# Projections and shared maxima of a decoder block's main loop in two 64-row phases, beside score halves of the other row half

## The chip, the cores and the metric

One Trainium2 chip, one core of it. The metric is the device time of one execution in microseconds (us); less is better. Before the change the median of 3 runs is 760.02 us (757.07 to 762.93).

## The reference

A decoder block on `x` (32 batches, 56 tokens, 128 features) with a context of 32 x 1500 x 128:

```python
x = layernorm(x + linear_attention(x))
x = layernorm(x + cross_attention(x, ctx))
x = layernorm(x + ffn(x))

qh = (q @ Wq.T + bq)   # 16 heads of 8
kh = (k @ Wk.T + bk)
vh = (v @ Wv.T + bv)
scores = qh @ kh.T / sqrt(8)
out = softmax(scores) @ vh
```

Nearly all the time goes to the cross attention: for each of 32 batches, 1500 keys are projected to K and V, and 16 heads x 56 queries meet 1500 keys.

## The kernel before

The first stage (up to some 135 us) does the linear attention of all batches and, beside it, the K and V of the first batches. Then comes the **main loop**, one body for each of the 32 batches b; bodies 0 and 1 and the last two stand alone, the 28 between are a hardware loop of 14 passes, two bodies (u = 0, then u = 1) in each. A last stage does the feed-forward part.

In body b TensorE (PE) does, in a written-out order of six **steps** m = 0..5:

- **Scores** (line 1066) of batch b: 12 key tiles of 125 keys, two in each step. The 16 heads are stored in two halves of 64 partitions, so a tile is 4 pairs of matmuls: 64 rows x 128 columns of weights, 112 moving columns, one of the pair on the upper and one on the lower 64 rows of the array, at the same time. ScalarE (ACT) takes the exponent (line 756) of each half of a tile (4 x 112 columns) from one of three PSUM banks into `probs`.
- **PV** (lines 1083 and 1089): `probs` times V in fp32, in tiles of 128 x 32, two key tiles at the end of each step, one step late.
- **K2** (line 954), the projection of batch b + 2 to K: three units of 500 keys, each three fp16 matmuls of 128 rows and 500 columns (high and low parts of operands). ACT adds the bias (line 776, `k32`); GpSimd (POOL) casts it to fp16 (`kcast`, line 580) and forms the rest (`ksub`, line 586).
- **V** (line 962), the projection of batch b + 1 to V: three units, each 12 fp16 matmuls of 128 rows and 128 columns; ACT copies (line 765).
- **Maxima** (line 974): products of q and K whose row maxima VectorE (DVE) takes (line 1313, 672 ns each). There are 21 for each batch: 12 of the last ones of batch b + 1 ("M1") and 9 of the first ones of batch b + 2 ("M2"). A maximum is 500 columns; six of the seven row blocks need 64 rows only, and these go in pairs on the two row halves; the middle block (`SHARED`, r = 3) needs all 128 rows.
- **X** (line 978): turns the maxima; they are placed into `q_diag` by DMA before the next body's scores. In bodies with u = 0 there are also **T, Z, Y** (lines 982, 986, 989), which finish the output of the two batches before.

K2, V, maxima, X, T, Z and Y write into a **ring** of four PSUM banks in the order of the table `PLAN`; before a unit is written, PE waits until the unit that last held the bank has been read (`release`, line 942). A score of tile t waits for the exponents of tile t - 1's first half (line 1062), since there are three score banks.

POOL's order in a body (line 653): split chunks 0 and 1 of the context of b + 2 into high and low parts (`split`, line 557), `diag_q` of b + 1, chunk 2, `kcast` 0, `max_q` of b + 2, `kcast` 1 and 2, three `ksub`. The splits of b + 2 begin when the last V of batch b has been formed, since that used the same buffer.

SyncE (SP) moves K through DRAM into its stacked form (`store_k`, `load_k`), places the maxima and loads the context.

A PE matmul's tile is 64 x 128 for scores and unshared maxima, 128 x 128 for K2, V, shared maxima, T, Z and Y, and 128 x 32 for PV.

Of the kernel before, what the change touches and what calls it, by code (L numbers as in the profile page):

```python
# [34 lines left out]
ACT = mybir.ActivationFunctionType  # L35
# [62 lines left out]
def settle(engine, counter):  # L98
# [13 lines left out]
U1_SHIFT = 3  # L112
LATE_STACK = 4
PAIR_KINDS = ("T", "Z", "Y")
VW = 48
M_ORDER = ((3, 0), (0, 0), (4, 0), (1, 0), (5, 0), (2, 0), (6, 0), (0, 1), (4, 1), (1, 1), (5, 1), (3, 1),
           (2, 1), (6, 1), (0, 2), (4, 2), (1, 2), (5, 2), (3, 2), (2, 2), (6, 2))
PAIRS = (1, 3, 5, 7, 9, 12, 14, 16, 19)
SHARED = MB // 2
PLAN = ((("M1", "M1", "M1", "K2"), ("M1", "M1"), ()),  # L120
        (("M1", "M1", "V"), ("M1", "M1"), ()),
        (("M1", "K2", "M1", "M1"), (), ()),
        (("M2", "K2", "X"), ("M2", "M2", "T"), ()),
        (("V", "Z"), ("M2", "M2"), ()),
        (("M2", "M2", "V", "Y"), ("M2", "M2"), ()))
O_COPY = (0, 1)

def unit_plan(u):

    made = {"M1": EARLY_M}
    steps = []
    for parts in PLAN:
        step = []
        for kinds in parts:
            units = []
            for kind in kinds:
                if kind in PAIR_KINDS and u:
                    continue
                units.append((kind, made.get(kind, 0)))  # L140
                made[kind] = made.get(kind, 0) + 1
            step.append(units)
        steps.append(step)
    assert made["M1"] == NM and made["M2"] == EARLY_M and made["V"] == made["K2"] == KC
    return steps
# [7 lines left out]
def ring_slots():  # L153

    rounds = [[unit for step in unit_plan(u) for part in step for unit in part] for u in range(2)]
    return [{unit: (k + u * U1_SHIFT) % RING for k, unit in enumerate(units)} for u, units in enumerate(rounds)]

def left_in_ring(slots, u, s1, s2, before):

    left = {}
    for (kind, i), slot in slots[u].items():
        if active(kind, s1, s2, before):
            left[slot] = (kind, i)
    return left
# [76 lines left out]
def decoder_block(nc, ctx_dram, x_dram, pack_dram, out_dram, m):  # L242
# [4 lines left out]
    plans = [unit_plan(u) for u in range(2)]  # L247

    with ExitStack() as stack:
# [89 lines left out]
        init, o_zeroed = sem("init"), sem("o_zeroed")  # L339
        INIT = 2 + 4  # L340
# [33 lines left out]
        with nc.Block() as block:  # L374
# [125 lines left out]
            def _(pool):  # L500
# [204 lines left out]
            def _(act):  # L705
# [44 lines left out]
                def exp(b, t):  # L750
                    for half in range(2):
                        k = 2 * t + half
                        act.wait_ge(s_ready, b * 2 * KT + k + 1)
                        if half == 0:
                            wait_past(act, pv_done, b * KT + t - PBUF + 1)
                        nc.scalar.activation(probs[0:KP, t % PBUF, half * 2 * GC:(half + 1) * 2 * GC],  # L756
                                             scores[k % RING_AT][0:KP, 0:2 * GC], ACT.Exp, scale=SCALE).then_inc(p_ready, 1)

                def v_copy(n, i, u, bank):
                    act.wait_ge(ready["V"], n * 3 + i + 1)  # L760
                    if i == 0:
                        wait_past(act, pv_done, (n - 1) * KT)
# [43 lines left out]
                def body(b, u, s1, s2):  # L806

                    def copies(units):
                        for kind, i in units:
                            bank = ring[slots[u][kind, i]]  # L810
                            if kind == "V" and s2:
                                v_copy(b + 1, i, 1 - u, bank)
                            if kind == "X" and s2:
                                m_copy(b + 1, bank)
                            if kind == "K1" and s2:
                                k_copy(b + 1, i, bank)
                            if kind == "K2" and s1:
                                k_copy(b + 2, i, bank)

                    for m, (one, two, three) in enumerate(plans[u]):  # L820
                        exp(b, 2 * m)
                        if not s2 and 2 * m in X2T_STEPS:
                            x2_T(X2T_STEPS.index(2 * m))
                        copies(one)
                        exp(b, 2 * m + 1)
                        copies(two + three)
# [32 lines left out]
            def _(pe):  # L859
# [88 lines left out]
                def unit(kind, i, n, u, bank, before):  # L948
# [15 lines left out]
                    elif kind in ("M1", "M2"):  # L964
                        r, c = M_ORDER[i]
                        if i % MB == 0:
# [90 lines left out]
                def score(b, t, u):  # L1057
                    if t == 0:
# [3 lines left out]
                    wait_past(pe, p_ready, b * 2 * KT + 2 * t - 1)  # L1062
                    for g in range(G):
                        for half in range(2):
                            rows = slice(HALF * half, HALF * half + HALF)
                            mm = nc.tensor.matmul(scores[(2 * t + half) % RING_AT][:, g * PAIR:(g + 1) * PAIR],  # L1066
                                                  k_stack[u][rows, g, t * KP:t * KP + P],
                                                  q_diag[u][rows, g * PAIR:(g + 1) * PAIR], start=True, stop=True)
                            if g == G - 1:
                                mm.then_inc(s_ready, 1)  # L1070

                def pv(b, t, u):
# [6 lines left out]
                    pe.wait_ge(p_ready, b * 2 * KT + 2 * t + 2)  # L1079
# [17 lines left out]
                def body(b, pair, u, s1, s2, before, held):  # L1097
# [3 lines left out]
                    def go(units):  # L1101
                        for kind, i in units:
                            if active(kind, s1, s2, before):
                                n, slot = of_batch(kind, b, pair), slots[u][kind, i]
                                if kind in ("M1", "M2") and i in PAIRS:
                                    release(held[slots[u][kind, i + 1]])
                                unit(kind, i, n, u if kind in ("K2", "M2") else 1 - u, ring[slot], held[slot])
                                held[slot] = (kind, i, n)

                    for m, (one, two, three) in enumerate(plans[u]):  # L1110
                        score(b, 2 * m, u)
                        if not s2 and 2 * m in X2T_STEPS:
                            x2_T(X2T_STEPS.index(2 * m))
                        go(one)
                        score(b, 2 * m + 1, u)
                        go(two)
# [6 lines left out]
                        go(three)  # L1123
# [64 lines left out]
            def _(dve):  # L1188
# [211 lines left out]
                def body(b, pair, u, s1, s2, before):  # L1400

                    def reduce(units):
                        for kind, i in units:
# [141 lines left out]
```

## Time and profile before

| | |
|---|---|
| median of 3 runs | 760.02 us (757.07 to 762.93) |
| profiled execution, span from first to last instruction | 747.8 us |
| around the span (median less span) | 12.2 us |
| PE busy / DVE / ACT / POOL | 90% / 78% / 73% / 63% |
| mean granted TensorE clock | 0.970 |
| two bodies in the steady part of the loop | 35.19 us |

The profiled execution's own time is not given beside its span; the median less the span stands for what lies around it. Busy counts the time from a matmul's start to its modelled end, so PE at 90% need not be PE at its peak: how far apart the starts of matmuls stand tells more. A line number is that of the listing above.

### The profile page before, as it was taken

How to read it: one execution, taken by the hardware profiler on the slowest of the kernel's cores; microseconds unless marked ns; L12 is line 12 of the kernel's file. 1: busy time of each engine (PE TensorE's matmuls, PEld its weight loads, DVE VectorE, ACT ScalarE, POOL GpSimd, SP SyncE). 2: the span in 40 equal slices, each digit the busy share in tenths (PEclk: the TensorE clock that was granted, in tenths of full speed). 3: DMA queues.
4: the chain of work that ended last, by engine and by line, in shares of the span. 5: the costliest groups of instructions: out<-in, count | busy, mean ns of one | idle time of the engine just before them, and what ended most of it. 6: DMA issues, size and time to landing. Idle time of an engine off the chain costs nothing.

```text
span 747.8 us, 33172 instructions
## 1 busy us (share of the span) xinstructions
PE 672.6 (90%) x12468; PEld 431.4 (58%) x12468; DVE 586.6 (78%) x1139; ACT 548.7 (73%) x1123; POOL 471.6 (63%) x507
## 2 busy tenths in 40 slices
PE   6779864999899999999999999999999999998883
PEld 3456531566566666666666666666666666666553
DVE  5768976887588888888887878888788888885597
ACT  4537523788688888888888888888788888887751
POOL 6625424477477777777676777667777777723464
PEclk9989986899999999999999999999999999999997
DMA  7203402579767767687877776777767677761001
GB/s 217 83 2 101 89 16 81 88 172 210 148 103 151 179 142 148 146 164 145 160 146 155 151 145 144 145 166 150 180 155 150 144 160 150 127 109 15 1 1 49
DMA packets 39405, 93.20 MB, mean 125 GB/s; under 512 B 7880, under 2 KB 14536, under 8 KB 39368
## 3 DMA queue, kind: packets, MB, share of 16 engines
q1 hardware_dynamic: 39368, 92.69, 59.1%
q8 instruction: 25, 0.41, 0.3%
q14 instruction: 12, 0.10, 0.1%
HBM read 66.06 MB, written 26.54 MB: 124 GB/s over the span
## 4 chain that ended last, share of the span: by engine, by line
PE 70%; DVE 14%; issue 7%; ACT 6%; DMA 1%; POOL 1%; ACTq 0%; DVEq 0%; POOLq 0%
PE psum L1066 13%; PE psum L1083 12%; PE psum L974 11%; PE psum L962 10%; PE psum L1089 9%; DVE mx L1313 5%; PE psum L954 4%; ACT probs L756 3%; PE psum L905 2%; ACT k L776 1%; DVE rden L1241 1%; PE psum L891 1%; PE psum L982 1%; PE psum L920 1%; DVE k_stack L1452 1%
## 5 line engine op out<-in xcount | busy, mean ns | idle before, releaser
L1313 DVE TENSOR_REDUCE mx<-psum 128x1 f32<-128x500 f32 x672 | 423.8, 673 | 85.8 <-PE psum L974 83.5
L756 ACT ACTIVATE probs<-psum 125x448 f32<-125x448 f32 x768 | 376.0, 544 | 85.9 <-PE psum L1066 84.7
L974 PE MATMUL psum<-kh,q_max 64*128 64x500 f16 (+1 forms) x672 | 149.0, 383 | 15.0 <-DVE mx L1313 14.9
L1083 PE MATMUL psum<-probs,v_ext 125*32 125x112 f32 x3072 | 149.3, 266 | 0.5 <-issue 0.5
L1066 PE MATMUL psum<-q_diag,k_stack 64*128 64x112 f16 x3072 | 143.0, 212 | 3.3 <-ACT probs L756 2.2
L1089 PE MATMUL psum<-probs,v_ext 125*32 125x112 f32 x3072 | 144.6, 260 | 0.0
L580 POOL CAST kh<-k 128x500 f16<-128x500 f32 x96 | 57.9, 603 | 120.4 <-ACT k L776 112.0
L1066 PEld LDWEIGHTS psum<-q_diag,k_stack 64*128 64x128 f16 x3072 | 85.0, 95 | 67.8 <-ACT probs L756 38.7
L568 POOL TENSOR_TENSOR c_hl<-c_in,c_hl 128x500 f16<-128x500 f32 x96 | 110.6, 1152 | 7.7
L586 POOL TENSOR_TENSOR kl<-k,kh 128x500 f16<-128x500 f32 x96 | 107.4, 1148 | 0.0
L1083 PEld LDWEIGHTS psum<-probs,v_ext 125*32 125x32 f32 x3072 | 74.1, 109 | 38.8 <-issue 26.0
L566 POOL CAST c_hl<-c_in 128x500 f16<-128x500 f32 x96 | 60.0, 625 | 47.4 <-PE psum L962 44.5
L1089 PEld LDWEIGHTS psum<-probs,v_ext 125*32 125x32 f32 x3072 | 87.3, 110 | 0.0
L962 PE MATMUL psum<-WvH,c_hl 128*128 128x128 f16 x768 | 76.1, 221 | 0.0
L974 PEld LDWEIGHTS psum<-kh,q_max 64*128 64x128 f16 (+1 forms) x672 | 39.2, 94 | 61.8 <-DVE mx L1313 35.8
L962 PE MATMUL psum<-WvL,c_hl 128*128 128x128 f16 x384 | 69.5, 219 | 3.3 <-issue 3.3
L776 ACT ACTIVATE k<-psum,pack 128x500 f32<-128x500 f32 x96 | 65.1, 679 | 7.5 <-PE psum L954 6.2
L962 PEld LDWEIGHTS psum<-WvH,c_hl 128*128 128x128 f16 x768 | 55.7, 98 | 20.5 <-DVE mx L1313 15.4
L765 ACT COPY v_ext<-psum 125x512 f32<-125x512 f32 x96 | 56.7, 590 | 4.0 <-PE psum L962 4.0
L954 PE MATMUL psum<-c_hl,WkH 128*128 128x500 f16 x192 | 56.6, 376 | 0.5 <-ACT mT L771 0.3
L607 POOL TENSOR_TENSOR q_max<-qh,pack 128x896 f16<-128x896 f32 (+1 forms) x32 | 54.1, 1691 | 1.4 <-ACT qh L747 1.4
L962 PEld LDWEIGHTS psum<-WvL,c_hl 128*128 128x128 f16 x384 | 37.8, 98 | 3.5 <-issue 3.5
(143 smaller groups left out, 681.2 us busy)
## 6 DMA issues: line engine op xcount, KB each, us to landing
k_stack<-k_halves SPq DMA_DIRECT2D x192, 187.5 KB, 6.3
c_in<-ctx_in SPq DMA_DIRECT2D x32, 750.0 KB, 5.2
k_halves<-kh SPq DMA_DIRECT2D x32, 375.0 KB, 4.8
k_halves<-kl SPq DMA_DIRECT2D x32, 375.0 KB, 5.5
q_stack<-q_halves SPq DMA_DIRECT2D x32, 64.0 KB, 2.4
q_diag<-mT SPq DMA_DIRECT2D x64, 0.8 KB
q_diag<-mT SPq DMA_DIRECT2D x64, 0.1 KB
out<-x_all SPq DMA_DIRECT2D x8, 112.0 KB
```

The costliest lines, as they stand in the source:

```text
L566: nc.gpsimd.tensor_copy(c_hl[:, buf, 0, keys], c_in[:, buf, keys]).then_inc(c_hi, 1)
L568: nc.gpsimd.tensor_tensor(c_hl[:, buf, 1, keys], c_in[:, buf, keys], c_hl[:, buf, 0, keys], ALU.subtract).then_inc(c_split, 1)
L586: nc.gpsimd.tensor_tensor(kl[u][:, keys], k32[:, keys], kh[u][:, keys], ALU.subtract).then_inc(kl_done, 1)
L756: nc.scalar.activation(probs[0:KP, t % PBUF, half * 2 * GC:(half + 1) * 2 * GC], scores[k % RING_AT][0:KP, 0:2 * GC], ACT.Exp, scale=SCALE ...
L776: nc.scalar.activation(k32[:, i * CH:(i + 1) * CH], bank[:, 0:CH], ACT.Identity, bias=w("bk")).then_inc(k32_done, 1)
L954: last = nc.tensor.matmul(bank[:, 0:CH], wt[:, :], c_hl[:, u, part, i * CH:(i + 1) * CH], start=(k == 0), stop=(k == 2))
L962: last = nc.tensor.matmul(bank[:, j * P:(j + 1) * P], c_hl[:, u, part, at:at + P], wt[:, :], start=(k == 0), stop=(k == 2))
L974: last = nc.tensor.matmul(bank[:, 0:CH], q_max[u][rows, r * P:(r + 1) * P], kh[u][rows, c * CH:(c + 1) * CH], start=True, stop=True)
L1066: mm = nc.tensor.matmul(scores[(2 * t + half) % RING_AT][:, g * PAIR:(g + 1) * PAIR], k_stack[u][rows, g, t * KP:t * KP + P], q_diag[u][ro ...
L1083: nc.tensor.matmul(O[32 * j:32 * j + 32, 0:2 * N], v_ext[u][0:KP, v:v + 32], probs[0:KP, t % PBUF, at:at + 2 * N], start=(t == 0), stop=(t ...
L1089: last = nc.tensor.matmul(O[32 * j:32 * j + 32, 2 * N:GC], v_ext[u][0:KP, v:v + 32], probs[0:KP, t % PBUF, at + 2 * N:at + GC], start=Fals ...
L1313: dve.tensor_reduce(mx[:, r * KC + c:r * KC + c + 1], bank[:, 0:CH], AX.X, ALU.max).then_inc(mx_done, 1)
```

## The change

Everything that was 128 rows deep in the loop, but for X, T, Z, Y and PV, is cut into two phases of 64 rows. A K2 unit is 3 matmuls on the upper 64 rows (phase 0) and 3 on the lower (phase 1), accumulating in one bank; a V unit 12 and 12; a shared maximum 1 and 1. While such a phase holds one row half, the other row half holds four score matmuls or a maximum. Scores change from "two halves of one tile" to "one half of two tiles": in step m, scores j = 0 and 1 are the lower half of tiles 2m and 2m + 1, scores j = 2 and 3 their upper half. New semaphores `k_low`, `v_low`, `m_high` make phase 1 wait for phase 0.

Each step holds exactly one projection unit: V0, K2 0, K2 1, K2 2, V1, V2 (`UNITS_OF`). Steps 0 to 2 hold four M1 maxima each, steps 3 to 5 two unshared and one shared M2 maximum each. X goes from the middle of step 3 to its end. Ring bank 0 holds projections alone, banks 1 to 3 the maxima and T, Z, Y, X.

The tables:

```diff
+UNITS_OF = (("V", 0), ("K2", 0), ("K2", 1), ("K2", 2), ("V", 1), ("V", 2))
+def maxima_of(m):
+    if m < M1_STEPS:
+        at = EARLY_M + 4 * m
+        return "M1", (at, at + 1, at + 2, at + 3)
+    at = 3 * (m - M1_STEPS)
+    return "M2", (at, at + 2, at + 1, at + 2)
...
+        table = {unit: 1 + k % (RING - 1) for k, unit in enumerate(ring_users(u))}
+        table["X", 0] = table[maxima_of(X_STEP)[0], maxima_of(X_STEP)[1][2]]
+        table.update({unit: 0 for unit in UNITS_OF})
```

GpSimd's body:

```diff
+                        max_q(b + 2, u)
                         kcast(b + 2, 0, u)
-                        max_q(b + 2, u)
                         kcast(b + 2, 1, u)
+                        ksub(b + 2, 0, u)
                         kcast(b + 2, 2, u)
-                        ksub(b + 2, 0, u)
```

ScalarE's body:

```diff
+                    for m in range(KT // 2):
+                        kind, i = UNITS_OF[m]
+                        if m == X_STEP + 1 and s2:
+                            m_copy(b + 1, ring[slots[u]["X", 0]])
+                        exp(b, m, 0)
+                        exp(b, m, 1)
+                        exp(b, m, 2)
+                        if kind == "V" and s2:
+                            v_copy(b + 1, i, 1 - u, ring[0])
+                        if kind == "K2" and s1:
+                            k_copy(b + 2, i, ring[0])
...
+                        exp(b, m, 3)
```

TensorE:

```diff
+                def score(b, m, j, u, g):
+                    k, t, half = 4 * m + j, 2 * m + j % 2, 1 - j // 2
...
+                    if g == 0:
+                        wait_past(pe, p_ready, b * 2 * KT + k - 2)
...
+                def k_part(n, i, u, half, part):
+                    rows = slice(HALF * half, HALF * half + HALF)
+                    wt, of = ((WkH, 0), (WkH, 1), (WkL, 0))[part]
...
+                    if half == 1 and part == 0:
+                        pe.wait_ge(k_low, (n - 2) * KC + i + 1)
+                    mm = nc.tensor.matmul(ring[0][:, 0:CH], wt[rows, :], c_hl[rows, u, of, i * CH:(i + 1) * CH],
+                                          start=(half == 0 and part == 0), stop=(half == 1 and part == 2),
...
+                    def beside_score(m, j, half, part, kind, i, live):
+                        for g in range(G):
+                            if live and kind == "V":
+                                v_part(b + 1, i, 1 - u, half, 4 * part + g)
+                            if live and kind == "K2" and g == 0:
+                                k_part(b + 2, i, u, half, part)
+                            score(b, m, j, u, g)
...
+                    for m in range(KT // 2):
...
+                        if live:
+                            own(kind, i)
+                        beside_score(m, 0, 0, 0, kind, i, live)
+                        bank = own(top, one) if counted else None
+                        beside_maximum(0, 1, kind, i, live, top, one, bank)
+                        beside_score(m, 1, 0, 2, kind, i, live)
+                        if counted:
+                            second = own(top, two)
+                            maximum(b + 1 if top == "M1" else b + 2, two, 1 - u if top == "M1" else u, 1, second)
+                        for g in range(G):
+                            score(b, m, 2, u, g)
+                        bank = own(top, three) if counted else None
+                        beside_maximum(1, 0, kind, i, live, top, three, bank)
+                        beside_score(m, 3, 1, 1, kind, i, live)
...
+                            bank = own(top, four)
+                        beside_maximum(1, 2, kind, i, live, top, four, bank)
...
                         if m:
                             pv(b, 2 * m - 2, u)
                             pv(b, 2 * m - 1, u)
```

`beside_maximum(half, part, ...)` issues the next third of the projection (one `k_part`, or four `v_part`) with one maximum on the other row half behind its first matmul; `own` is `release` and the note of who holds the bank. VectorE takes the maxima in the order in which PE forms them, `o_copy` at the end of step 0, T, Z and Y behind the maxima of steps 3, 4 and 5.

What PE's rows look like in a step with a K2 unit, before (the loop's first body, from the scores of tile 4 to PV; lines of the listing above; REGISTER_ALU works out what a wait is for):

```order
L1066 MATMUL psum<-q_diag,k_stack 128x112 x8
L946 REGISTER_ALU
L974 MATMUL psum<-kh,q_max 128x500
L946 REGISTER_ALU
L952 REGISTER_ALU
L954 MATMUL psum<-c_hl,WkH 128x500 x2
L954 MATMUL psum<-c_hl,WkL 128x500
L946 REGISTER_ALU x2
L974 MATMUL psum<-kh,q_max 128x500 x2
L90 REGISTER_ALU
L1066 MATMUL psum<-q_diag,k_stack 128x112 x8
L1079 REGISTER_ALU
```

And after, the first part of such a step (L1107 is K2, L1093 the scores, L1143 a maximum):

```order
L1104 REGISTER_ALU
L1107 MATMUL psum<-c_hl,WkH 128x500
L90 REGISTER_ALU
L1093 MATMUL psum<-q_diag,k_stack 128x112 x4
L972 REGISTER_ALU
L1107 MATMUL psum<-c_hl,WkH 128x500
L1143 MATMUL psum<-kh,q_max 128x500
L1107 MATMUL psum<-c_hl,WkL 128x500
L90 REGISTER_ALU
L1093 MATMUL psum<-q_diag,k_stack 128x112 x4
L972 REGISTER_ALU
L1143 MATMUL psum<-kh,q_max 128x500
```

The three K2 matmuls no longer follow each other: each is now a 64-row one and has four scores or a maximum behind it on the other row half, and a step reads one K2 unit twice in this way.

POOL at the end of a body of the loop, before (L568 is a split, L580 `kcast`, L607 `max_q`, L586 `ksub`):

```order
L568 TENSOR_TENSOR c_hl<-c_in,c_hl 128x500
L90 REGISTER_ALU x2
L580 CAST kh<-k 128x500
L607 ISA
L607 TENSOR_TENSOR q_max<-qh,pack 128x896
L580 CAST kh<-k 128x500 x2
L586 TENSOR_TENSOR kl<-k,kh 128x500 x3
```

And after (L599 a split, L638 `max_q`, L611 `kcast`, L617 `ksub`):

```order
L599 TENSOR_TENSOR c_hl<-c_in,c_hl 128x500
L635 REGISTER_ALU
L638 ISA
L638 TENSOR_TENSOR q_max<-qh,pack 128x896
L90 REGISTER_ALU
L611 CAST kh<-k 128x500 x2
L617 TENSOR_TENSOR kl<-k,kh 128x500
L611 CAST kh<-k 128x500
L617 TENSOR_TENSOR kl<-k,kh 128x500 x2
```

`max_q` now stands ahead of the first `kcast`, and one `ksub` between the second and the third.

## Rows read from the trace of the kernel before

**Rows 1.** The page: the chain that ended last, shares by engine

```profile
PE 70%; DVE 14%; issue 7%; ACT 6%; DMA 1%; POOL 1%; ACTq 0%; DVEq 0%; POOLq 0%
```

**Rows 2.** Windows, one pass of the loop: us, busy (x records) by engine, PEclk

```profile
375.49:392.33 16.84, 16.62 (x356) 10.77 (x355) 13.82 (x25) 14.68 (x32) 12.68 (x14) 1.00 0.68 147
392.33:410.68 18.35, 17.69 (x363) 11.43 (x363) 14.84 (x30) 14.80 (x32) 12.69 (x14) 1.00 0.79 154
```

**Rows 3.** Waits in that pass, longest of ACT: who for whom, total us, times, longest

```profile
ACT probs L756 <- PE psum L1066: 5.3, 12, 1.1
```

**Rows 4.** Timeline, PE in a step with V: start, us, line, form, count

```profile
404.05 0.37 PE L1066 MATMUL psum<-q_diag,k_stack 64*128 64x112 f16 x8
...
404.26 0.37 PE L974 MATMUL psum<-kh,q_max 64*128 64x500 f16 x2
...
404.57 0.28 PE L962 MATMUL psum<-WvH,c_hl 128*128 128x128 f16 x2
...
405.19 0.22 PE L962 MATMUL psum<-WvL,c_hl 128*128 128x128 f16 x1
...
405.34 0.37 PE L1066 MATMUL psum<-q_diag,k_stack 64*128 64x112 f16 x8
...
405.55 0.37 PE L974 MATMUL psum<-kh,q_max 64*128 64x500 f16 x2
...
405.85 0.40 PE L1083 MATMUL psum<-probs,v_ext 125*32 125x112 f32 x8
...
406.76 0.37 PE L1066 MATMUL psum<-q_diag,k_stack 64*128 64x112 f16 x8
```

**Rows 5.** Timeline, PE around a K2 unit

```profile
401.02 0.69 PE L974 MATMUL psum<-kh,q_max 64*128 64x500 f16 x3
...
401.55 0.58 PE L954 MATMUL psum<-c_hl,WkH 128*128 128x500 f16 x2
...
401.97 0.37 PE L954 MATMUL psum<-c_hl,WkL 128*128 128x500 f16 x1
...
402.28 0.37 PE L1066 MATMUL psum<-q_diag,k_stack 64*128 64x112 f16 x8
```

**Rows 6.** Timeline, ACT: exponents, K2's copy, V's copy

```profile
402.38 0.68 ACT L776 ACTIVATE k<-psum,pack 128x500 f32<-128x500 f32 x1
...
402.96 0.97 ACT L756 ACTIVATE probs<-psum 125x448 f32<-125x448 f32 x2
...
404.53 0.98 ACT L756 ACTIVATE probs<-psum 125x448 f32<-125x448 f32 x2 [0.60 <-PE psum L1066]
...
405.45 0.59 ACT L765 COPY v_ext<-psum 125x512 f32<-125x512 f32 x1
...
405.93 0.99 ACT L756 ACTIVATE probs<-psum 125x448 f32<-125x448 f32 x2
```

**Rows 7.** Timeline, DVE: maxima one after another

```profile
401.43 3.08 DVE L1313 TENSOR_REDUCE mx<-psum 128x1 f32<-128x500 f32 x5 [0.17 <-PE psum L974]
```

**Rows 8.** Timeline, POOL: a split, diag_q, the next split, kcast, max_q

```profile
400.83 0.60 POOL L566 CAST c_hl<-c_in 128x500 f16<-128x500 f32 x1
...
402.61 0.94 POOL L595 TENSOR_TENSOR q_diag<-q_stack,pack 128x448 f16<-128x448 f32 x1
...
403.49 0.60 POOL L566 CAST c_hl<-c_in 128x500 f16<-128x500 f32 x1
...
405.25 0.60 POOL L580 CAST kh<-k 128x500 f16<-128x500 f32 x1
...
405.81 1.69 POOL L607 TENSOR_TENSOR q_max<-qh,pack 128x896 f16<-128x896 f32 x1
```

**Rows 9.** Timeline, PE in the loop's first pass; the page's queue of instruction packets

```profile
200.04 0.23 PE L962 MATMUL psum<-WvL,c_hl 128*128 128x128 f16 x1 [3.33 <-issue]
...
q8 instruction: 25, 0.41, 0.3%
```

**Rows 10.** The DMA queues between 220 and 660 us, all instruction packets

```profile
q14 instruction: 2, 0.02, 0.0%
```

More of the change, by code:

```diff
@@ L126 @@
[L126 to L145, printed above, removed]
+HIGH_ORDER = ((4, 0), (5, 0), (6, 0), (4, 1), (5, 1), (6, 1), (4, 2), (5, 2), (6, 2))
@@ new lines, with ring_users @@
+M_ORDER = maxima_order()
+CHUNK_FIRST = tuple(min(i for i in range(NM) if M_ORDER[i][1] == c) for c in range(KC))
+def maxima_of(m):
[4 more added lines that the diff above has]
+    return "M2", (at, at + 2, at + 1, at + 2)
+def ring_users(u):
+    users = []
+    for m in range(KT // 2):
+        kind, (one, two, three, four) = maxima_of(m)
+        users += [(kind, one), (kind, two), (kind, three)]
+        if four != two:
+            users.append((kind, four))
+        if u == 0 and m in (T_STEP, Z_STEP, Y_STEP):
+            users.append((("T", "Z", "Y")[m - T_STEP], 0))
+    return users
@@ L1099, in body @@
                     held = dict(held)
[L1101 to L1108, printed above, removed]
@@ L1110, in body, with own @@
-                    for m, (one, two, three) in enumerate(plans[u]):
-                        score(b, 2 * m, u)
+                    def own(kind, i):
+                        slot = slots[u][kind, i]
+                        release(held[slot])
+                        held[slot] = (kind, i, of_batch(kind, b, pair))
+                        return ring[slot]
+                    def beside_score(m, j, half, part, kind, i, live):
[5 more added lines that the diff above has]
+                            score(b, m, j, u, g)
@@ new lines, in beside_maximum @@
+                    def beside_maximum(half, part, kind, i, live, top, at, bank):
+                        n, of = (b + 1, 1 - u) if top == "M1" else (b + 2, u)
+                        if live and kind == "V":
+                            v_part(b + 1, i, 1 - u, half, 4 * part)
+                        if live and kind == "K2":
+                            k_part(b + 2, i, u, half, part)
+                        if bank is not None:
+                            maximum(n, at, of, 1 - half, bank)
+                        for g in range(1, G):
+                            if live and kind == "V":
+                                v_part(b + 1, i, 1 - u, half, 4 * part + g)
@@ new lines, in body @@
+                    for m in range(KT // 2):
+                        kind, i = UNITS_OF[m]
+                        live = active(kind, s1, s2, before)
+                        top, (one, two, three, four) = maxima_of(m)
+                        counted = active(top, s1, s2, before)
+                        if live:
[12 more added lines that the diff above has]
+                        beside_score(m, 3, 1, 1, kind, i, live)
+                        if not counted:
+                            bank = None
+                        elif four == two:
+                            bank = second
+                        else:
+                            bank = own(top, four)
+                        beside_maximum(1, 2, kind, i, live, top, four, bank)
@@ L1112, in body @@
                         if not s2 and 2 * m in X2T_STEPS:
                             x2_T(X2T_STEPS.index(2 * m))
-                        go(one)
-                        score(b, 2 * m + 1, u)
-                        go(two)
+                        for last_of, name in ((T_STEP, "T"), (Z_STEP, "Z"), (Y_STEP, "Y")):
+                            if m == last_of and u == 0 and before:
+                                slot = slots[u][name, 0]
+                                unit(name, 0, pair - 1, 0, ring[slot], held[slot])
+                                held[slot] = (name, 0, pair - 1)
@@ L1400, in body @@
                 def body(b, pair, u, s1, s2, before):
[L1402 to L1406 removed]
+                    for m in range(KT // 2):
+                        top, (one, two, three, four) = maxima_of(m)
+                        for i in sorted({one, two, three, four}):
+                            if top == "M1" and s2:
+                                m_max(b + 1, i, ring[slots[u][top, i]])
                                 if i == NM - 1:
```

173 lines of the change are left out of this document (100 added, 73 removed).

## The prediction

> **What bounds the kernel now.** I read the page's chain first, then windows over one pass of the loop, then the waits, and last the timeline of each engine in one step. The chain runs 70% through PE [rows 1]. A pass of the loop (two bodies) takes 16.84 + 18.35 = 35.19 us, the same in pass after pass, and PE shows busy in nearly all of it, while ACT and DVE show 14 to 15 us in each body and POOL 12.7 [rows 2]. ACT's longest wait is for PE's scores [rows 3]: the other engines wait for PE.
>
> "Busy" hides what PE loses, so look at the starts. Two K2 matmuls stand 0.42 us before the third, 0.21 each for 500 columns [rows 5]; eight scores in pairs take 404.05 to 404.26, 0.21; the twelve V matmuls start every (405.19 - 404.57) / 11 = 0.056 [rows 4]. But from a pair of maxima (500 columns) to the first V matmul it is 404.26 to 404.57, 0.31; from the last V matmul to the scores 405.19 to 405.34, 0.15; from a pair of maxima to PV 405.55 to 405.85, 0.30 [rows 4]; from the last K2 matmul to the scores 0.31 [rows 5]. Each is 0.09 to 0.10 longer than the matmul before it needs. Scores to maxima, both tiles of 64 x 128, lose nothing (404.26 is just when eight scores have been streamed). So every change of tile shape costs some 0.095, and a step has four of them: PV to scores, scores to the 128-row unit, back, and to PV. The profile names them "issue" or nothing. The clock stands at 1.00 of its upper level (2.4 GHz) throughout [rows 2], so that is not what costs.
>
> **The change part by part, for one pass (two bodies).**
>
> *Shape changes.* Before: 24 in the steps of a body and one more for X, twice, and one for T: 51 in a pass. After: K2, V and all maxima have the scores' shape, and a step keeps two (PV to 64 rows and back): 24 in a pass. T, Z and Y now add one each; X, whose tile is 128 x 32 like PV's, stands behind PV and adds none. That makes 27, or 24 fewer: 24 x 0.095 = -2.3 us.
>
> *The work between PVs.* Before, in a body: 12 tiles of scores x 0.21, 9 pairs of maxima x 0.21, 3 shared x 0.21, 9 K2 matmuls x 0.21, 36 V matmuls x 0.056 = 2.52 + 1.89 + 0.63 + 1.89 + 2.02 = 8.95 [rows 4, 5]. After, a step is seven phases in which both row halves work. With K2 a phase is 500 columns beside 500, or beside four scores of 0.05: 7 x 0.21 = 1.47. With V, six phases hold four V matmuls, 4 x 0.056 = 0.225, and one a maximum beside scores: 6 x 0.225 + 0.21 = 1.56. Three of each: 9.1. So cutting depth in two buys nothing by itself, since twice as many matmuls stand two abreast: +0.15 a body, +0.3 a pass. A PV block with the change of shape behind it is 405.85 to 406.76, 0.91 [rows 4], as before. A K2 step then takes 1.47 + 0.09 + 0.91 = 2.47, a V step 2.56, six of them 15.1.
>
> *Waits.* Before: 8.95 + 6 x 0.91 + 19 other changes of shape x 0.095 + X 0.06 = 16.3 of the 16.84 of the body without T, Z, Y: about 0.6 a body is waiting. After, two waits come in its place.
> (1) The fourth maximum of steps 0 to 2 uses the bank of the first. The first starts 0.21 into the step, DVE begins 0.41 later (401.02 to 401.43 [rows 5, 7]) and needs 0.67 (five in a row take 3.08, some 0.60 each and a tail [rows 7]): 1.29, against 1.26 when PE wants the bank, and some tenth for the signal. That is 0.1 to 0.2 in three steps. Behind the waiting maximum PE holds the rest of the projection and both PVs, so all is delayed.
> (2) The projections have one bank, so the next step can't begin before ACT has copied. An exponent starts 0.48 after its scores (404.05 [rows 4], 404.53 [rows 6]), two take 0.92 (404.53 to 405.45), V's copy 0.59 and K2's 0.68 [rows 6]. Three exponents end at 0.48 + 3 x 0.46 = 1.86; V's copy at 2.45, before the 2.56 that PE needs; K2's at 2.54, after 2.47: 0.1 with its signal, where (1) has not already used it up. For a step ACT needs 4 x 0.46 + 0.68 = 2.5 at most, so it has little left, but enough.
> Together 0.4 to 0.7 a body. I take 0.6, as before: nothing. Ends: -0.8 a pass if both waits vanish, +0.9 if each comes in every step.
>
> *POOL.* V moves to steps 0, 4 and 5, K2 to 1, 2 and 3, and `max_q` ahead of the first `kcast`. From the last V matmul (step 5) POOL needs two chunks of 1.78 (400.83 to 402.61), diag_q 0.88, a chunk 1.76, max_q 1.69 and a cast 0.60 [rows 8]: 8.5 us, and PE wants the cast in step 3's first maximum, 1.0 + 7.5 to 7.9 + 0.2 = 8.7 to 9.1 later. It is hidden by 0.2 to 0.6 only. I cost it at nothing; uncovered, its upper end is some 0.5 a body.
>
> *SP and DMA.* The same transfers. X is one third of a step later; `place_m` still has two steps to land. Nothing.
>
> *Matmuls of different length side by side.* No row shows this: pairs so far have equal lengths. Lower bound nothing (two streams that don't know of each other, as the eight scores suggest); upper bound below, in the third rival. I take nothing, since the rows nearest to it, scores and maxima of one shape, lose nothing at the seam.
>
> *Ends of the program.* The last body has no unit to put beside its scores: 16 matmuls at 0.05 in a step instead of 8 pairs, +0.4 a step at most; ACT's exponents (1.84 a step) cover most of it. +1 us.
>
> *Sum.* -2.3 + 0.3 + 0 = -2.0 a pass, or 1.0 a body; 30 bodies have units: -30, +1. The profiled span of 747.8 and the 12.2 around it make 760.0, which is the median: **731 us**. With the ends of the waits and POOL (-2.8 to -1.1 a pass): 718 to 744.
>
> **Rivals.**
>
> 1. *POOL or the single projection bank takes over.* For it: POOL's margin of 0.2 to 0.6 and ACT's of nothing in K2 steps, both worked out from rows of an unhurried kernel. Against: POOL waits in the trace as it is, and PE's own waits before were as large. At +1.0 a pass the gain halves: 745.
>
> 2. *The loop's code no longer stays in PE's instruction memory, and each pass waits for code: slower.* In the first pass PE stood still for 3.33 us in the middle of a V unit, for nothing but issue [rows 9]. That the 25 packets of queue q8 (0.41 MB, 16 KB each [rows 9]) are PE's code I infer from its moments; between 220 and 660 us there are none of q8 at all [rows 10], so the loop's code is kept. A pass has 719 matmul records and 718 of weight loads [rows 2]; the change adds 48 matmuls a body, 96 + 96 a pass, 13%. If that is past what is kept, a page at the loop's head is dropped and fetched anew at each jump back: 13 jumps x 3.4 = +44, or **775**; it decides when the pass, from the page it begins in to the page fetched ahead behind its end, needs one page more than there is. For it: the stall is real and the loop is long. Against: nothing tells from the rows how much room is left.
> The Trainium skill's "Runtime: NRT & Kernel Launch", section "Instruction fetch mechanics", gives PE's memory as 2048 instructions in blocks of 256, refilled in order, and a fetch where a branch's target has left it. The absent q8 packets agree with a loop that is held. By that figure I estimate that the 1437 records become 1629, with the instructions for waits some 1800: still under 2048, but with a block begun at the head and a block fetched ahead it is tight.
>
> 3. *Unequal matmuls side by side don't run freely.* If a matmul may not end before the one issued ahead of it, four scores behind a K2 matmul end at 0.21 + 3 x 0.05 = 0.36 instead of 0.21: four such phases in a K2 step (+0.6), one in a V step (+0.15), and in three V phases the matmuls behind a maximum end 0.1 later: +0.6 + 0.45 = 1.05 for two steps, 3.1 a body, 6.3 a pass; less the waits that it covers, 5: 15 x (5 - 2.0) = +45, or **805**. It decides from the first body on. Against: nothing in the rows hints at it; pairs start together, and the seam from scores to maxima is free [rows 4].
> The Trainium skill's "TensorE: Matmul & The Clock Gate", section "Part 3: Packing small matmuls", says that matmuls start and end strictly in the order of the program. No run here shows it for unequal lengths; taken at its word it gives this rival, and if it only holds signals back, it costs nothing.
>
> **How the numbers follow.** As forecast 0.55, rival 1 0.14, rival 2 0.19, rival 3 0.12. A measurement of this kernel tells about 1% (7.6 us) from no change. Faster by more: all of the forecast and two thirds of rival 1, 0.65. Within 1%: the rest of rival 1 and a quarter of rival 2, 0.10. Slower: 0.25. The range reaches from 715 to 782, over rival 2 with its own spread; left out are rival 3 and little else. The forecast's own range is 718 to 744.
>
> **What would show it.** Right: a pass of 32.4 to 34.1 us; no gap but PV's two in a step; a K2 phase 0.21, a V phase 0.225. Rival 1: a maximum or score that waits for POOL's cast in step 3, or the step's first K2 or V matmul for ACT's copy, by over 0.3. Rival 2: q8 packets between 220 and 660 us and a gap of 3 us in each pass. Rival 3: K2 phases of 0.36. The forecast is wrong if shape changes from 64 to 64 rows on other halves cost as much as those counted, or if the pass does not shorten by 1.1 us at least.

## The result and the profile after

The changed kernel takes 988.02 us (median of 6 runs, 979.91 to 1008.79) against 755.09 of the kernel before beside it: 1.303 times as long, 95% interval 1.296 to 1.310. That ratio counts fast runs alone: two of the six, the profiled one among them, were over 1.5% above the fastest. The kernel is slower, and far outside the range of 715 to 782. The page of the kernel after (the profiled execution is the longest of the six, 1008.79 us):

```profile
span 1007.0 us, 36435 instructions
...
PEclk9899669797979697969797978879797879699697
...
q8 instruction: 144, 2.36, 1.2%
...
PE 57%; issue 17%; DVE 13%; POOL 5%; DMA 4%; ACT 2%; SPq 1%; POOLq 0%; DVEq 0%; ACTq 0%
```

Against [rows 1] the chain has lost PE and gained "issue", time in which an engine waits for nothing that the profile shows; queue q8 has 144 packets instead of the 25 of [rows 9]. Between 220 and 880 us it has 113, where the kernel before has none between 220 and 660 [rows 10]. One pass, from X to X (windows; columns as in [rows 2]):

```profile
427.82:462.55 34.73, 21.55 (x407) 17.06 (x408) 15.75 (x28) 15.40 (x32) 13.57 (x16) 0.75 0.45 88
462.55:481.72 19.17, 17.02 (x414) 13.25 (x405) 14.59 (x28) 14.87 (x31) 11.84 (x14) 1.00 0.61 131
sum 53.90, PE 38.56 PEld 30.30 DVE 30.34 ACT 30.27 POOL 25.41; mean PE 19.28 PEld 15.15 DVE 15.17 ACT 15.14 POOL 12.70
```

It is 53.90 us instead of the 35.19 of [rows 2]. DVE, ACT and POOL are busy about as long as before: they wait for PE. PE's clock is at 1.00 in one body and at a mean of 0.75 in the other, so part of that body ran at the lower level (1.2 GHz). In PE's timeline of this pass four gaps of over 1.5 us stand out. They are shown with the rows ahead of them (start, duration, engine, line, operation, what the idle time is put down to):

```profile
430.92 0.22 PE L1125 MATMUL psum<-WvL,c_hl 64*128 64x128 f16 x1
433.52 0.39 PE L1125 MATMUL psum<-WvH,c_hl 64*128 64x128 f16 x2 [2.31 <-issue]
...
436.96 0.36 PE L1168 MATMUL psum<-probs,v_ext 125*32 125x112 f32 x8
442.97 0.28 PE L1125 MATMUL psum<-WvH,c_hl 64*128 64x128 f16 x1 [5.64 <-POOL c_hl L599]
...
445.81 0.31 PE L1125 MATMUL psum<-WvL,c_hl 64*128 64x128 f16 x1
450.55 0.60 PE L1143 MATMUL psum<-kh,q_max 64*128 64x500 f16 x1 [4.43 <-issue]
...
472.53 0.36 PE L1093 MATMUL psum<-q_diag,k_stack 64*128 64x112 f16 x4
474.82 0.38 PE L1107 MATMUL psum<-c_hl,WkL 64*128 64x500 f16 x1 [1.94 <-DVE mx L1441]
```

From the start of the last matmul ahead of the gap to the start of the next one, the four are 2.60, 5.90, 4.74 and 2.15 us. The first and the third stand in the middle of a V phase, as the one stop of [rows 9] did. The second is at the loop's jump back. The profile names POOL there, but POOL's operation (441.40, 1.13 long) had ended 0.4 before, while PE's sequencer stood in the jump itself: the record of the branch begins at 436.35 and lasts 6.30. Here are all the jumps of this run, and below them those of the padded kernel of experiment 1 (a_aligned); the three numbers are the shortest, the median and the longest in ns, and the shortest is the last one, which leaves the loop:

```profile
L1296 PEldq COMPARE_BRANCH  x14: 83/7430/8487, 226.2 to 915.0; - x14
```
```profile
L1299 PEldq COMPARE_BRANCH  x14: 76/208/246, 225.2 to 680.9; - x14
```

The 13 jumps back take 6.3 to 8.5 us each, 96 together, where the padded loop's take 0.21 to 0.25 and no packet of q8 falls between 250 and 640 us. So this too is a stop for code. The fourth gap is in the middle of a K2 step; the profile names DVE there, whose maximum had ended 0.96 before. The pass has 9 packets of q8.

### The profile page after: what moved, and what is told of

It reads as the page before. It is cut to its first block, busy times and chain, and to the rows that moved or that the text cites. A ratio compares the mean times of both kernels' runs of the same rounds, so it can differ in the third digit from the quotient of the medians.

```text
span 1007.0 us, 36435 instructions
## 1 busy us (share of the span) xinstructions
PE 751.0 (75%) x13944; PEld 561.8 (56%) x13944; DVE 606.4 (60%) x1139; ACT 560.7 (56%) x1123; POOL 472.2 (47%) x507
## 4 chain that ended last, share of the span: by engine, by line
PE 57%; issue 17%; DVE 13%; POOL 5%; DMA 4%; ACT 2%; SPq 1%; POOLq 0%; DVEq 0%; ACTq 0%
PE psum L1125 10%; PE psum L1093 10%; PE psum L1162 9%; PE psum L1143 7%; PE psum L1168 7%; PE psum L1107 6%; DVE mx L1441 5%; POOL c_hl L599 2%; DMA k_halves<-kl 2%; POOL c_hl L597 2%; PE psum L931 1%; DMA k_stack<-k_halves 1%; DVE rden L1369 1%; PE psum L917 1%; POOL q_diag L626 1%
## 5 line engine op out<-in xcount | busy, mean ns | idle before, releaser
L1143 PE MATMUL psum<-kh,q_max 64*128 64x500 f16 x732 | 291.8, 421 | 25.0 <-issue 24.8
L1093 PE MATMUL psum<-q_diag,k_stack 64*128 64x112 f16 x3072 | 279.6, 227 | 26.2 <-issue 23.2
L1125 PE MATMUL psum<-WvH,c_hl 64*128 64x128 f16 x1488 | 169.4, 232 | 105.9 <-issue 94.7
L1093 PEld LDWEIGHTS psum<-q_diag,k_stack 64*128 64x128 f16 x3072 | 205.0, 103 | 56.2 <-issue 38.2
L611 POOL CAST kh<-k 128x500 f16<-128x500 f32 x96 | 57.7, 601 | 314.8 <-ACT k L807 314.8
L1125 PEld LDWEIGHTS psum<-WvH,c_hl 64*128 64x128 f16 x1488 | 117.4, 101 | 130.2 <-issue 108.2
L1125 PE MATMUL psum<-WvL,c_hl 64*128 64x128 f16 x744 | 151.5, 233 | 1.6 <-issue 1.6
L1107 PE MATMUL psum<-c_hl,WkH 64*128 64x500 f16 x360 | 121.8, 422 | 0.8 <-ACT v_ext L796 0.7
L599 POOL TENSOR_TENSOR c_hl<-c_in,c_hl 128x500 f16<-128x500 f32 x96 | 109.7, 1142 | 7.7
L617 POOL TENSOR_TENSOR kl<-k,kh 128x500 f16<-128x500 f32 x96 | 108.5, 1145 | 0.0
L1107 PE MATMUL psum<-c_hl,WkL 64*128 64x500 f16 x180 | 77.2, 429 | 36.2 <-issue 29.3
L1143 PEld LDWEIGHTS psum<-kh,q_max 64*128 64x128 f16 x732 | 74.2, 101 | 36.9 <-issue 34.3
L1125 PEld LDWEIGHTS psum<-WvL,c_hl 64*128 64x128 f16 x744 | 76.7, 103 | 1.9 <-issue 1.8
```

Of the source, the lines that this page charges most:

```text
L599: nc.gpsimd.tensor_tensor(c_hl[:, buf, 1, keys], c_in[:, buf, keys], c_hl[:, buf, 0, keys], ALU.subtract).then_inc(c_split, 1)
L617: nc.gpsimd.tensor_tensor(kl[u][:, keys], k32[:, keys], kh[u][:, keys], ALU.subtract).then_inc(kl_done, 1)
L1093: mm = nc.tensor.matmul(scores[k % RING_AT][:, g * PAIR:(g + 1) * PAIR], k_stack[u][rows, g, t * KP:t * KP + P], q_diag[u][rows, g * PAIR: ...
L1107: mm = nc.tensor.matmul(ring[0][:, 0:CH], wt[rows, :], c_hl[rows, u, of, i * CH:(i + 1) * CH], start=(half == 0 and part == 0), stop=(half ...
L1125: mm = nc.tensor.matmul(ring[0][:, j * P:(j + 1) * P], c_hl[rows, u, of, at:at + P], wt[rows, :], start=(half == 0 and x == 0), stop=(half ...
L1143: mm = nc.tensor.matmul(bank[:, 0:CH], q_max[u][rows, r * P:(r + 1) * P], kh[u][rows, c * CH:(c + 1) * CH], start=(r != SHARED or half == ...
```

## The experiments

**1. Where the loop lies in PE's code.** Empty instructions ahead of PE's first matmul move the loop without changing it:

```diff
+                for _ in range(109):
+                    settle(pe, pe_pad)
                 pe.wait_ge(pack_first, 16)
```

> The changed kernel with 109 empty PE instructions ahead of its first matmul, where PE waits for the first load anyway; the loop is the same, but begins 109 instructions later in the code and so at the head of a 16 KB block (counted from where PE stood still in the loop's first pass before the change). Code theory: the loop then lies in one block less, no q8 packets fall between 220 us and the loop's end, a pass takes 32 to 34 us and the time 725 to 745 us. Rival, the new order itself is slow (unequal matmuls, the single projection bank) and the code packets are a side effect: within 1% of 988 us.

> The kernel before with 30 empty PE instructions ahead of its first matmul; nothing in the loop differs. Counted in the same way, its loop then lies in 8 blocks of code instead of 7. Code theory: over 100 q8 packets, a pass of 45 to 60 us instead of 35.2, and 880 to 1000 us. Rival: 755 us within 1%.

> The kernel before with 60 empty PE instructions ahead of its first matmul: its loop begins early in a block and lies in 7 blocks again. Both theories: 755 us within 1%, 25 or 26 q8 packets. If it is slow as well, it is the empty instructions and not the blocks that cost.

> The changed kernel with 60 empty PE instructions ahead. By the count of the program the loop then touches eight blocks and ends some 200 instructions into the eighth, well past its middle; a_pad100, where the code was kept although the count gave 3 instructions in a first block, then says that the count is off by a few. Theory 1 (eight kept, a ninth fetched ahead once PE is past the middle of the eighth): passes of 50 to 54 us, 970 to 1020 us, over 100 q8 packets. Theory 2 (any padding of this size helps): 762 to 772 us, 27 packets.

> The changed kernel with 100 empty PE instructions ahead, nine fewer than a_aligned. By the count of the program the loop then begins 3 instructions before a block's border and ends 240 into its eighth block. Theory 1 (eight blocks are kept, and a ninth is fetched ahead once PE is past the middle of the eighth): the code is fetched in every pass, passes of 50 to 54 us, 980 to 1020 us, over 100 q8 packets. Theory 2 (the padding helped in some other way, by what it delays): as a_aligned, 765 to 775 us, under 30 packets.

> The changed kernel with 120 empty PE instructions ahead, eleven more than a_aligned. By the count of the program the loop then touches eight blocks but ends 4 instructions into the eighth. Theory 1 (a ninth block is fetched only past the middle of the eighth): nothing is fetched in the steady passes, passes of 35.0 us, 770 to 777 us, under 32 q8 packets. Theory 2 (eight blocks in the loop are one too many, whatever their filling): passes of 50 to 54 us, 980 to 1020 us, over 100 packets.

Measured: the changed kernel with 109 empty instructions takes 772.15 us (ratio to before 1.017, 1.008 to 1.026) with 27 packets of q8, and its pass is 35.01:

```profile
395.43:413.28 17.85, 17.00 (x407) 13.38 (x408) 15.38 (x28) 15.12 (x32) 13.59 (x16) 1.00 0.77 150
413.28:430.44 17.16, 16.97 (x415) 13.18 (x406) 14.55 (x28) 14.76 (x31) 11.79 (x14) 1.00 0.77 151
sum 35.01, PE 33.96 PEld 26.56 DVE 29.93 ACT 29.88 POOL 25.38; mean PE 16.98 PEld 13.28 DVE 14.97 ACT 14.94 POOL 12.69
```

With 100 and 120 it takes 767.28 and 783.16 (one run each), 27 packets, a pass of 35.0. With 60 it takes 1038.19 (one run), 144 packets, and passes like the unpadded kernel's (the one from 420.69 to 474.14):

```profile
sum 53.45, PE 37.98 PEld 29.20 DVE 30.32 ACT 30.11 POOL 25.46; mean PE 18.99 PEld 14.60 DVE 15.16 ACT 15.05 POOL 12.73
```

The kernel before, moved by 30 and 60, stays at 760.59 and 762.11 (ratios 1.003 and 1.004, both intervals hold 1). So the same instructions in the same order cost some 270 us more or less by their place alone, and that is shown (1038.19 with 60, 767.28 with 100). One rule fits all of it, though it is inferred: eight blocks are kept; the next block is fetched ahead once PE is well into the last one it has; when loop and block ahead are nine, every block is gone when its turn comes again. Unpadded and with 60, the loop touches eight and ends beyond the middle of the eighth (140 and 200 in). With 107 and 109 it touches seven; with 120, and in the kernel before moved by 30, eight, but it ends near the start of the eighth. Of the expectations on which loops refetch, two missed: the kernel before moved by 30 was to refetch, by a rule without the block ahead, and the one with 100 was to refetch, by 3 instructions, which is finer than the count. The one with 109 missed by size: a pass of 32 to 34 us and 725 to 745 us were expected, and experiments 3 and 4 look for the rest. The times with 60 and 120 also lie above what was expected for them, by 18 and 6 us. At what point in a block the fetch begins was not tried.
The Trainium skill's "Runtime: NRT & Kernel Launch", section "Instruction fetch mechanics", gives 2048 instructions for PE in blocks of 256, that is eight blocks; these runs agree.

**2. The loop written out.** The same changed kernel, PE's 14 passes in line:

```diff
-                with pe.Fori(1, B // 2 - 1) as i:
+                for i in range(1, B // 2 - 1):
```

> The changed kernel with PE's 14 passes written out one after the other: no jump back, the code is read once in order. Code theory: some 100 blocks more are read, nearly all of them ahead of need as in the bodies that stand before the loop (one stop of 3.3 us in 11 blocks there): 730 to 790 us. Rival: some 988 us.

Measured: 878.03 us (ratio 1.160, 1.149 to 1.171), 81 packets of q8 between 220 and 760 us. The 730 to 790 expected was missed: code read in order isn't free either, and about half of the loss stays. The refetching loop pays 110 us on top, and its 13 jumps take 96.

**3. The padding's own cost.** 107 empty instructions, where PE waits for DVE anyway (20 ahead of `attend` 1, 15 ahead of the last `out_projection`, 36 ahead of each of the last two `x1_T`):

```diff
                 def x1_T(q):
+                    if q >= QUADS - 2:
+                        rest(36)
```

> The changed kernel with 107 empty PE instructions as in a_aligned, but put where PE waits for DVE anyway (20, 15, 36 and 36 ahead of four waits of the first stage), not ahead of its first matmul. Theory 1: 12 us of a_aligned's time are its own padding (its first matmul comes at 17.44 us, 5.59 in the changed kernel), so 757 to 763 us, first X 3 to 8 us later than in the kernel before, passes of 35.0 us. Theory 2: what a_aligned lost early is code that PE fetches in the straight bodies and the first pass: 768 to 773 us, first X 10 us later or more.

Measured: 760.26 us, ratio 1.004 (0.999 to 1.008); passes of 35.01. The median is 11.9 us below experiment 1's, where 109 empty instructions put off PE's first matmul from 5.59 to 17.44 us, 0.109 each: of the two theories the first gave the time. But at the last X the two traces differ by 4.8 only (692.04 and 687.26), so how much of the 11.9 is padding isn't settled. X's first came 8.5 us later than before, and from there to the sixth X it took 114.3 us, before 105.1 (216.38 - 111.27): theory 2's loss is there too. In that stretch PE's waits name three stops for code of 1 us or more, 7.1 together, instead of the one of 3.3 in [rows 9]. And the padding isn't all hidden: PE stands 4.9 at the last `x1_T`, where it waits 3.7 in the unpadded kernel:

```profile
PE psum L1180 <- issue: 5.0, 2, 3.9
PE psum L973 <- issue: 4.9, 1, 4.9
PE psum L1174 <- issue: 2.1, 1, 2.1
```

**4. GpSimd's order.** With the code at rest the pass is 35.01, 0.18 less than before, not 2.0. The timelines of DVE and of POOL in a_spread show one reason:

```profile
475.57 0.17 DVE L1459 TENSOR_REDUCE mrow<-mx 128x7 f32<-128x21 f32 x1
475.78 1.13 DVE L1463 TENSOR_SCALAR m<-mrow 128x7 f16<-128x7 f32 x1
476.82 1.25 DVE L1453 TENSOR_REDUCE mx<-psum 128x1 f32<-128x500 f32 x2
```
```profile
475.18 0.61 POOL L612 CAST kh<-k 128x500 f16<-128x500 f32 x1 [0.60 <-ACT k L808]
475.74 1.14 POOL L618 TENSOR_TENSOR kl<-k,kh 128x500 f16<-128x500 f32 x1
```

`m`, the scaling of 7 numbers a lane that X waits for, takes 1.13 us; in the kernel before it is 0.17 in all 32 bodies. It begins 0.04 after POOL's `ksub` 0 and ends with it (476.91 and 476.88), and so it goes in every body of the steady passes (1.07 to 1.13). In the kernel before, POOL stood idle at that time, between `kcast` 1 and 2. Two kernels, one for each direction: a_spread with `ksub` 0 behind `kcast` 2 again, and the kernel before with GpSimd's new order alone.

```diff
                         kcast(b + 2, 1, u)
-                        ksub(b + 2, 0, u)
                         kcast(b + 2, 2, u)
+                        ksub(b + 2, 0, u)
```

> a_spread with one line of GpSimd's body back where it was: ksub 0 behind kcast 2. Theory 1: in the new order DVE's subtraction that ends the row maxima (m, 173 ns in the kernel before) runs at the same moment as POOL's ksub 0 and waits for it (1.07 and 1.13 us, both end together), which delays X, the maxima of step 3 and T: m back at 0.17 to 0.6 us, a pass 33.4 to 34.3 us instead of 35.01, 10 to 20 us less than a_spread (738 to 752). Theory 2: PE's own steps set the pass and the long m is hidden: m short again, but the pass stays within 0.2 of 35.0 and the time within 3 us of a_spread.

> The kernel before with GpSimd's new order alone (max_q ahead of kcast 0, ksub 0 ahead of kcast 2). Theory 1 (DVE's m waits for a POOL operation that began before it): in the kernel before m stands in POOL's idle time between kcast 1 and 2; now ksub 0 is there, m takes 0.5 to 1.1 us instead of 0.17 and X comes later, a pass 35.6 to 37.0 us instead of 35.19, 6 to 25 us slower. Theory 2 (m's long time is DVE's own, from the order of the maxima): m 0.17, pass 35.2, same time.

Measured: without the collision `m` is 0.17 again, and the pass is 33.90:

```profile
489.53 0.17 DVE L1463 TENSOR_SCALAR m<-mrow 128x7 f16<-128x7 f32 x1
```
```profile
474.70:491.42 16.72, 16.72 (x415) 13.25 (x406) 14.04 (x28) 14.38 (x31) 12.38 (x14) 1.00 0.81 158
491.42:508.60 17.18, 16.96 (x415) 13.32 (x407) 14.28 (x28) 15.33 (x33) 13.02 (x15) 1.00 0.85 164
sum 33.90, PE 33.68 PEld 26.57 DVE 28.32 ACT 29.71 POOL 25.40; mean PE 16.84 PEld 13.28 DVE 14.16 ACT 14.85 POOL 12.70
```

The kernel takes 752.04 us, 8.2 less than a_spread: ratio to the kernel before 0.991 (0.987 to 0.996). It is the one version here whose interval lies below 1, and its gain is 0.9%. The pass gave what theory 1 said; the time gave less than its 10 to 20, though 14 passes x 1.11 make 15.5. Part of the rest was lost ahead of the steady passes, where X's first five intervals are 118.5 us here and 114.3 in a_spread: PE's waits there name 12.3 us of stops for code of over 1 us, in a_spread 7.1. In the other direction the kernel before with GpSimd's order is 10.5 us slower: 767.38, ratio 1.011 (1.007 to 1.015). Its pass is 35.68 instead of 35.19, which makes 6.9 over 14 passes. The rest fits the stretch ahead of the steady passes, where its trace has 7.5 us of stops for code instead of 3.3, so it isn't shown to come from `m`. In the steady passes `m` takes 0.75 or 0.83 beside a `ksub`:

```profile
313.11 0.75 DVE L1323 TENSOR_SCALAR m<-mrow 128x7 f16<-128x7 f32 x1
```
```profile
312.69 1.13 POOL L586 TENSOR_TENSOR kl<-k,kh 128x500 f16<-128x500 f32 x1
```

**5. V in full depth.** The new order with V as it was, 12 matmuls of 128 rows between two pairs of phases (the maxima of V steps change sides, and ACT copies V one exponent earlier), and `ksub` 0 behind `kcast` 2:

```diff
+                        if kind == "V":
+                            for j in range(4):
...
+                                    maximum(n_max, at, of, j // 2, bank)
+                                for g in range(G):
+                                    score(b, m, j, u, g)
+                                if j == 1 and live:
+                                    unit("V", i, b + 1, 1 - u, ring[0], held[0])
```

> The changed kernel with V in full depth again (12 matmuls of 128 rows between two pairs of phases; the maxima of the V steps change sides for it) and GpSimd's ksub 0 behind kcast 2; K2 and the rest of the new order stay; no padding. By the count of the program the loop has 1629 PE instructions instead of 1779 and touches seven blocks. Theory 1 (cutting V bought nothing: the two changes of shape it saves, 0.19, are spent on the wait of phase 1 for phase 0): nothing fetched in the steady passes, a V step 2.60 to 2.72 us, a pass within 0.5 of the 33.90 of a_spread_ksub, 742 to 754 us. Theory 2 (the prediction's: cutting V pays 0.1 or more in each V step): a V step 2.8 or more, a pass 34.5 or more, 756 to 766 us.

Measured: 756.85 us, ratio 0.999 (0.995 to 1.003), with no packet of q8 between 250 and 640 us and no padding (1629 instructions in the loop), but a pass of 35.19 (418.80 to 453.99):

```profile
sum 35.19, PE 35.04 PEld 26.68 DVE 28.54 ACT 29.71 POOL 25.34; mean PE 17.52 PEld 13.34 DVE 14.27 ACT 14.86 POOL 12.67
```

That is 1.29 a pass more than with V cut (33.90), 0.21 on average for each of six V units: theory 2. Step by step it runs from -0.02 to 0.45. The V steps without T, Z or Y take 2.77 to 3.02, in a_spread_ksub 2.65 to 3.02, and in the kernel before 2.52 to 2.76. So v_full's own order costs something as well, and what V's depth alone is worth isn't shown. The end of V in one such step on PE:

```profile
441.05 0.22 PE L990 MATMUL psum<-WvL,c_hl 128*128 128x128 f16 x1
441.20 0.38 PE L1146 MATMUL psum<-kh,q_max 64*128 64x500 f16 x1
```

The last V matmul and the next maximum stand 0.15 apart, where one V matmul needs 0.056: the 0.095 of a change of shape, once more.

## Why the prediction was wrong, step by step

**The forecast took the code for kept; rival 2 had the right cause and the wrong price.** The step that failed is that the sum has no term for code: it stands in rival 2 alone, with a chance of 0.19, and there as "a page at the loop's head is dropped and fetched anew at each jump back: 13 jumps x 3.4 = +44". Rival 2 named the condition correctly (a page begun at the head and one fetched ahead behind the end). But a pass fetches 9 packets, not one, as it must when blocks leave in the order in which they came and one too many drops every block just ahead of its use. Four stops, 2.6, 5.9, 4.7 and 2.2 us, make 15.4 of the 18.9 by which the pass is longer than a_aligned's. The rest fits the lower clock around them (a mean of 0.75, and PE busy for 38.56 us against 33.96), which no run takes apart. The jump alone, a median of 7.4, costs twice the 3.4. From a_spread's 760.26 to 988.02 it is 16.3 a pass over 14 passes, five times the 3.4. And rival 2's "against", that nothing tells how much room is left, was too quick: the program tells how long the loop is (1779, close to the estimated 1800), and by the block borders the change takes it from seven blocks to eight and over the middle of the last.

**POOL: "I cost it at nothing" failed**, though not as rival 1 had it. (The forecast's own range of 718 to 744 is that of the waits alone: POOL's upper end, 0.5 a body or 15 us in all, isn't in it, though the text says so.) The `kcast` that PE waits for was in time. What came was a wait of DVE for POOL, which no row of before shows because POOL stood idle there: 1.11 a pass (35.01 to 33.90). I followed who waits for POOL's results, not what runs beside it.

**The sum of -2.0 a pass** is -1.29 with both of these removed. For each V unit cut the steps of the prediction make it 0.14 (4 x 0.21 + 12 x 0.056 + 2 x 0.095 = 1.70 against 1.56); experiment 5's 0.21 has the same sign, but holds more than V's depth. The term that was mis-sized is the K2 step, 2.47. In the kernel before, a K2 step without T, X or a longer wait takes 2.67 (from PV to PV, 405.85 to 408.52), as by the prediction's prices, and in a_spread_ksub a K2 step without T takes 2.62 to 2.73: cutting K2 was to gain 0.2 a step, 1.2 a pass, and gained nothing there. One such step is 2.70 (485.20 to 487.90):

```profile
485.20 0.40 PE L1174 MATMUL psum<-probs,v_ext 125*32 125x112 f32 x8
...
486.13 0.38 PE L1119 MATMUL psum<-c_hl,WkH 64*128 64x500 f16 x1
486.24 0.32 PE L1105 MATMUL psum<-q_diag,k_stack 64*128 64x112 f16 x3
486.35 0.38 PE L1119 MATMUL psum<-c_hl,WkH 64*128 64x500 f16 x1
...
486.44 0.37 PE L1155 MATMUL psum<-kh,q_max 64*128 64x500 f16 x1
486.57 0.37 PE L1119 MATMUL psum<-c_hl,WkL 64*128 64x500 f16 x1
...
487.09 0.37 PE L1119 MATMUL psum<-c_hl,WkH 64*128 64x500 f16 x1
...
487.30 0.37 PE L1119 MATMUL psum<-c_hl,WkH 64*128 64x500 f16 x1
...
487.59 0.38 PE L1119 MATMUL psum<-c_hl,WkL 64*128 64x500 f16 x1
...
487.90 0.40 PE L1174 MATMUL psum<-probs,v_ext 125*32 125x112 f32 x8
```

A K2 phase is 0.21 to 0.22, as predicted. But the first scores start 0.11 after the first K2 matmul, not with it: a register's step and a wait of PE's sequencer stand between the two. The row half of the scores is then late through the whole of phase 0, and phase 1 needs it (487.09 instead of 486.98). Ahead of the last K2 matmul 0.08 goes to wait (1), DVE's bank, about as sized. Of the V steps without X, T, Z or Y two take 2.65, 0.1 over the 2.56, and one 3.02: phase 1 may start only when the last matmul of phase 0 has signalled. In a_aligned that is 431.21 to 431.58, 0.37, with only 0.21 of work beside it.

**Rival 1** (POOL's cast, the single projection bank) was not seen: no such wait in the pass of a_spread_ksub is over 0.2. **Rival 3** neither: its sign was K2 phases of 0.36, and they are 0.22 (486.13, 486.35, 486.57).

**The ends** cost more than the +1: from the first X to the sixth there are more stops for code than before, 7.1 us against 3.3 (experiment 3). And what lies around the span isn't 12.2 us: the run above that gives both numbers has 1.8 (1008.79 and 1007.0), so the profiled execution of before was some 10 us quicker than the median. The 731 started from the median, 760.0, so this cost the forecast nothing.

## What to carry to other kernels

Before a change lengthens a hardware loop's body, count the engine's instructions, waits and register steps included, and see where the loop begins and ends in its blocks: near the limit the same code costs nothing or a third of the time, by its place alone, and some padding in an idle stretch or a shorter body decides it. In a profile, look at how long the loop's branch takes (0.21 us or 7 here). Ask of a moved instruction not only who waits for its result but what it now runs beside: a 0.17 us step on the critical path can become 1.1. And where two row halves of PE work side by side, a wait at the head of one half's work (0.11 here) is paid where the halves meet (487.09 instead of 486.98).

## What the hardware showed that was not expected

Code read in order is not hidden here: the written-out loop lost 118 us on a_spread (878.03 against 760.26). The Trainium skill's "Runtime: NRT & Kernel Launch", section "Instruction fetch mechanics", calls the crossing of a block mostly hidden; in these runs the measurement differs.

DVE's `m` behaves as if it waited for POOL's whole operation: begun 0.04, 0.10, 0.33 and 0.41 us after a `ksub` it took 1.13, 1.07, 0.83 and 0.75, and ended with it, to 0.03. The row reductions beside POOL keep their 672 ns. The Trainium skill's "SBUF — State Buffer", section "SBUF: two separate sides", says that DVE and GpSimd share a pair of ports as an exclusive lock, which whoever starts first keeps for its whole instruction, where the DVE operation is in a 2-port mode or has two inputs in SBUF; the rows agree, though none shows which mode `m` runs in. That it is this lock was not tried otherwise than by moving `ksub`.
